# Causal masks of a forgetting attention on TensorE: mask rows loaded as weights, 64 streamed columns per mask matmul instead of 128

## The reference

```python
q = x @ Wq; k = short_conv(x @ Wk, kconv_w); v = short_conv(x @ Wv, vconv_w)   # 4 taps, then silu
q = group_rmsnorm(q, qnw, H); k = group_rmsnorm(k, knw, H)
cum = jnp.cumsum(jax.nn.log_sigmoid(x @ Wf + bf), axis=1)                      # per head
scores = jnp.einsum('bhtd,bhsd->bhts', qh, kh) * scale
scores = scores + (cum[:, :, :, None] - cum[:, :, None, :])
scores = jnp.where(causal, scores, -jnp.inf)
attn = jax.nn.softmax(scores, axis=-1)
out = jnp.einsum('bhts,bhsd->bhtd', attn, vh)
g = (x @ Wg).reshape(Bx, Tx, H, Dh)
out = out / rms(out) * onw * (g * jax.nn.sigmoid(g))
out = out.reshape(Bx, Tx, H * Dh) @ Wo
```

## Time and profile before

| | us |
|---|---|
| median of 3 runs | 2274.46 |
| lowest and highest | 2272.99, 2277.69 |
| span of the profiled execution, first to last instruction | 2273.2 |
| PE busy | 1915.3 (84 %) |
| DVE busy | 1508.8 (66 %) |
| ACT busy | 1375.1 (60 %) |
| POOL busy | 1002.6 (44 %) |

### The profile page before, as it was taken

One profiled execution on the slowest core, in us unless ns is written; L12 is line 12 of the kernel. 1 busy time (PEld: TensorE's weight loads), 2 busy tenths in 40 slices (PEclk: granted clock), 3 DMA queues, 4 the chain that ended last, 5 costly groups with the idle time before them and its releaser, 6 DMA issues. The chain is left out here.

```text
span 2273.2 us, 36182 instructions
## 1 busy us (share of the span) xinstructions
PE 1915.3 (84%) x11875; PEld 883.8 (39%) x11875; DVE 1508.8 (66%) x2281; ACT 1375.1 (60%) x2285; POOL 1002.6 (44%) x1110
## 2 busy tenths in 40 slices
PE   5468886686968758999999999999999857799996
PEld 2123333443654323444444444444444413222222
DVE  5979995794349677777778777787776536512122
ACT  3557773343344435766767767766765424699995
POOL 0167771561035314665665656656566631500001
PEclk9779997798979868999999999999999988899999
DMA  3000000000000011111121111111111100421210
GB/s 92 0 14 0 0 0 0 1 1 1 0 0 1 1 55 41 54 51 57 59 56 57 54 54 59 59 54 50 59 59 59 43 19 23 116 57 43 54 45 38
DMA packets 71430, 84.46 MB, mean 37 GB/s; under 512 B 20544, under 2 KB 44032, under 8 KB 71168
## 3 DMA queue, kind: packets, MB, share of 16 engines
q1 hardware_dynamic: 69536, 81.69, 12.3%
q10 hardware_dynamic: 1728, 0.67, 0.1%
HBM read 71.95 MB, written 9.57 MB: 36 GB/s over the span
## 5 line engine op out<-in xcount | busy, mean ns | idle before, releaser
L1690 DVE SCALAR_TENSOR_TENSOR fu_kv<-fu_ps_kv,fa_vec,fu_kv 128x511 f32<-128x511 f32 x366 | 252.8, 739 | 7.3 <-ACT fu_kv L1628 6.3
L2108 ACT ACTIVATE rt_p<-rt_ps_s 128x1024 f32<-128x1024 f32 x256 | 240.3, 1042 | 23.1 <-PE rt_ps_o L2053 17.8
L1769 POOL TENSOR_TENSOR fu_p<-fu_p 128x768 f32<-128x768 f32 x64 | 117.0, 1828 | 290.6 <-PE fu_ps_n L1475 285.4
L1445 PE MATMUL fu_ps_s<-fu_qn,fu_kn 64*128 64x512 f32 (+3 forms) x1024 | 190.9, 470 | 12.7 <-DVE fu_sg L1736 6.9
L1670 DVE TENSOR_REDUCE fu_nm<-fu_ps_m 128x2 f32<-128x1024 f32 x64 | 78.4, 1224 | 167.1 <-PE fu_ps_m L1468 167.1
L624 POOL TENSOR_TENSOR scan_hC<-scan_h,scan_c 128x1024 f32<-128x1024 f32 x64 | 150.9, 2358 | 71.7 <-DVE scan_h L600 71.7
L1475 PE MATMUL fu_ps_n<-fu_p,fu_vt 128*64 128x512 f32 (+3 forms) x1024 | 166.1, 445 | 0.0
L600 DVE TENSOR_TENSOR_SCAN scan_h<-scan_dA,scan_ps_b 128x1024 f32<-128x1024 f32 x64 | 146.4, 2287 | 2.2
L523 PE MATMUL scan_ps_y<-scan_hC,w_ident 128*128 128x512 f32 x256 | 125.5, 613 | 26.5 <-POOL scan_hC L624 14.9
L2053 PE MATMUL rt_ps_o<-rt_p,rt_va 128*32 128x512 f32 x1024 | 137.9, 610 | 10.5 <-ACT rt_p L2108 8.1
L1445 PEld LDWEIGHTS fu_ps_s<-fu_qn,fu_kn 64*128 64x128 f32 x1024 | 83.6, 186 | 133.0 <-issue 54.1
(11 more groups left out here) (368 smaller groups left out, 5037.2 us busy)
## 6 DMA issues: line engine op xcount, KB each, us to landing
fu_rb<-rms_rows SPq DMA_DIRECT2D x256, 128.0 KB, 3.0
fu_ro<-rms_rows SPq DMA_DIRECT2D x128, 128.0 KB, 2.9
ra_stackq<-rope_parts SPq DMA_DIRECT2D x168, 32.0 KB
ra_stackk<-rope_parts SPq DMA_DIRECT2D x168, 32.0 KB
w_X<-in_xT SPq DMA_DIRECT2D x4, 512.0 KB, 7.7
fa_wp<-in_wp SPq DMA_DIRECT2D x8, 256.0 KB
fa_cr<-ncum_rows SPq DMA_DIRECT2D x128, 3.0 KB
rope_parts<-ra_hi SPq DMA_DIRECT2D x16, 128.0 KB, 2.5
```

Source lines behind the costliest of these rows:

```text
L1445: pe.matmul(sps[:, h, at:at + T - t * P], k[head(h), t * P:(t + 1) * P], q[head(h), t * P:T], start=(at == 0), stop=False)
L1690: dve.scalar_tensor_tensor(acc, projected(a, k)[:, 0:T - j], vec[:, a % GA, at:at + 1], acc, ALU.mult, ALU.add).then_inc(done, 1)
L1769: pool.tensor_tensor(tail, tail, P13[:, :, 0:3 * P], ALU.add).then_inc(s.d1, 1)
L2108: act.activation(pr[k % 2][i][:, :, :], sps[(U * n + u) % RING][:, :, :], ACT.Exp, scale=DH_B ** -0.5).then_inc(s.exp, 1)
```

## The change

Before, a mask matmul loaded half an identity (64 rows, 128 columns) as weights and streamed 128 columns of mask rows. The result was a mask contribution of 128 rows and 128 columns, and the two halves j were added on the same 128 columns. Now it loads 64 mask rows (128 columns) as weights and streams an identity of 64 columns. The product is the transpose of those mask rows: 128 rows and 64 columns, so j = 0 fills the left half of the diagonal square and j = 1 the right one. As the product is transposed, `mask2` and `past2` change places.

```diff
@@ -1450,7 +1450,7 @@
                     for t, at in blocks:
                         for j in range(2):
                             for h in range(2):
-                                m = pe.matmul(sps[:, h, at:at + P], w.eye2[head(h), j, :], w.past2[head(h), j, :], start=False, stop=(j == 1 and t == blocks[-1][0]))
+                                m = pe.matmul(sps[:, h, at + 64 * j:at + 64 * j + 64], w.mask2[head(h), j, :], w.eye2[head(h), 0, 0:64], start=False, stop=(j == 1 and t == blocks[-1][0]))
                     m.then_inc(s.sc, 1)
@@ -1465,7 +1465,7 @@
                     for t, at in blocks:
                         for j in range(2):
                             for h in range(2):
-                                m = pe.matmul(mps[:, h, at + t * P:at + (t + 1) * P], w.eye2[head(h), j, :], w.mask2[head(h), j, :], start=False, stop=(j == 1 and t == blocks[-1][0]))
+                                m = pe.matmul(mps[:, h, at + t * P + 64 * j:at + t * P + 64 * j + 64], w.past2[head(h), j, :], w.eye2[head(h), 0, 0:64], start=False, stop=(j == 1 and t == blocks[-1][0]))
                     m.then_inc(s.mx, 1)
```

## The result

| us | before | changed |
|---|---|---|
| median (lowest to highest) of 4 runs each | 2275.14 (2272.99 to 2277.69) | 2261.82 (2257.86 to 2263.63) |
| span of the profiled execution | 2273.2 | 2261.1 |
| PE busy | 1915.3 | 1889.5 |
| A, median of 25 (iterations 6 to 54) | 15.628 | 15.306 |
| B, median of 26 | 14.3285 | 14.328 |

The ratio is 0.9942, with a 95% interval of 0.9924 to 0.9959: the changed kernel is faster, by 0.6 %. The two spans differ by 12.1: the stage began 2.7 later, took 12.4 less, and what lies behind it took 2.4 less. The forecast was 2262.2.

The account below looks back on a forecast made before the run. The prediction took A as bound by PE, then POOL and DVE, and B by ACT and DVE. Savings of 9.4 (A), 1.7 (first iterations) and 1.2 (last B) made 12.3 us, giving 2262.2, stated range 2254 to 2273.

Parts of the forecast that it names:

- A: Forgetting-attention iteration with output projection L1557, 15.62 us: bound by PE up to values product L1475, then by POOL and DVE.
- B: Forgetting-attention iteration between two A, without output projection, 14.33 us: bound by an ACT, then DVE chain ending at L1736.
- The price of a pair: Two mask matmuls, one per head, side by side: step time goes by streamed columns, so halving them saves 0.027 us.
- The floor: Mask steps: matmul starts at least about 25 ns apart; over both heads, 5 ns saved a pair, some 2.3 us altogether.
- A saves 12 pairs: In A, only the 12 pairs ahead of values product L1475 count: 0.32 us each, 9.4 over 29 iterations.
- B saves nothing: In B, PE arrives up to 0.43 us earlier at its end and waits for the same L1736: no saving.
- The sum: Whole attention stage: 9.4, 1.7 and 1.2 us add to 12.3 saved, taking the median to 2262.2.
- The first five iterations: Stage start: iterations 0, 1, 2 and 4 keep all 16 pairs, 4 x 0.43 = 1.7 us; 3 is like B.
- Iterations 56 to 62: Stage end: A saves 0.32 us each; B there follows POOL's chain and saves 0.3 each.
- An unchanged step: First rival, mask steps: a load or floor takes over, nothing saved, 2274.5 us; chance 0.15, a small saving included.
- a bound of PE alone: Second rival, whole stage: PE bounds everything, 64 x 0.43 = 27.6 us saved, 2246.9; chance 0.11.
- a load that waits for the drain: Third rival, mask steps: loads wait for their array half to drain, slower, about 2278 to 2361 us; chance 0.06.

Follow-up runs that it names:

- e3: Changed kernel with mask rows still as weights but the identity streaming 128 columns again: 2269.06 us, ratio 0.9993 to the kernel before.
- e4: Changed kernel with each mask matmul streaming 32 columns instead of 64, half of each diagonal square left unmasked: 2260.74 us, ratio 0.9943 to the kernel before.
- e1: Kernel before with only the score masks (L1453) narrowed to 64 columns: 2270.51 us, ratio 0.9984.
- e2: Kernel before with only the masks of the maxima (L1468) narrowed to 64 columns: 2264.53 us, ratio 0.9959.
- e12: Kernel before, old 128-column masks, with the same three moves as e11: 2298.26 us, ratio 1.0111.
- e11: Changed kernel with the moves of e8 and e9, and in B one tap behind two DVE reductions: 2280.16 us, ratio 1.0032 to the kernel before.
- e7: Changed kernel with ACT's mean squares behind its key and value copies and DVE's L1683 behind two taps: 2283.98 us, ratio 1.0051 to the kernel before.
- e5: Kernel before, old masks, with DVE's output scaling (L1719) moved right behind the queries' operation (L1677): 2265.89 us, ratio 0.9964.
- e6: Changed kernel with DVE's output scaling (L1719) moved right behind the queries' operation (L1677): 2260.55 us, ratio 0.9937 to the kernel before.
- e9: Changed kernel in which POOL, in A, waits for DVE's output scaling (L1719) before its last add (L1776): 2257.76 us, ratio 0.9935 to the kernel before.
- e8: Changed kernel with the output scaling moved behind the queries' operation in B only: 2263.3 us, ratio 0.9947 to the kernel before.

## Why the prediction was right, step by step

**The price of a pair: right.** Forecast 27 ns less; measured 27 from the records, and 0.427 of 16 pairs in each of iterations 1, 2 and 4. e3 shows that it is the columns. The floor that the third paragraph of the price took from a page of the Trainium skill ("TensorE: Matmul & The Clock Gate", "Wait — 56ns, not 53.3ns?") is near the 26 ns step of e4. Whether it or the load of 128 columns sets that step no run shows. It can't count over both heads, since both share one step of 29 ns, and so it left 27 of 27 ns here.

**A saves 12 pairs: right.** 0.322 measured, 0.32 forecast, by the chain given: POOL's wait fell by 0.32, L1719 ended 0.56 behind POOL, L1557 0.14 behind that. e1 and e2 split it into 6 and 6 pairs, and e12 against e11 shows the missing 4 come back when POOL's hold is gone. One detail was wrong: L1719 should have shrunk to 1.0, since DVE was to reach it at the old time. It kept 1.21, because L1712 ahead of it is held by POOL's L1773 in the same way (0.38, ending right behind it) and moved with POOL. In 2 of the 25 A the hold falls on the neighbour instead. One of them, DVE then PE:

```profile
1124.29 0.77 DVE L1714 TENSOR_TENSOR fa_mhl<-fu_nm,fa_mhl 128x8 bf16<-128x8 f32 x1
1124.96 0.85 DVE L1719 SCALAR_TENSOR_TENSOR fu_og<-fu_num,fu_ow,fu_ro 128x512 f32<-128x512 f32 x1
```

```profile
1125.95 1.10 PE L1557 MATMUL fu_ps_m<-fu_og,fa_wo 128*128 128x512 f32 x2 [0.37 <-DVE fu_og L1719]
```

L1776 started at 1124.28, 0.01 before L1714, which takes 0.20 elsewhere. L1719 starts 0.57 later than in the other A and ends 0.2 later, and that A takes 15.51.

**B saves nothing: right in size, wrong on where it would show.** 14.3285 and 14.328. The idle time put down to L1736 was to rise to 0.7; it stayed at 0.26, and the step from L1568 on at 0.66. PE gave its gain back earlier in B: the scores of block 2 wait for the exponential L1632, 6.86 into B where PE was ready at 6.70, and the maxima behind them wait for a reduction of DVE. Before and after:

```profile
1319.05 0.28 PE L1453 MATMUL fu_ps_s<-w_past,w_eye 64*128 64x128 bf16 x4
1319.40 0.28 PE L1461 MATMUL fu_ps_m<-fu_km,fu_qm 64*128 64x256 bf16 x2
```

```profile
1314.88 0.23 PE L1453 MATMUL fu_ps_s<-w_eye,w_mask 64*128 64x64 bf16 x4
1315.39 0.28 PE L1461 MATMUL fu_ps_m<-fu_km,fu_qm 64*128 64x256 bf16 x2 [0.29 <-DVE fu_nm L1700]
```

The maxima start 8.01 into B in all of these B of both kernels, so in the kernel before PE waited there already: from 1319.05 on are 0.35, where two mask steps take 0.11. I had looked only for the wait that ends B; there are three, and PE met the last two of them before the change and meets all three now. e7 makes the first of them bind the whole B, e5 and e6 free the chain behind it.

**The sum: 12.3 forecast, 12.4 in the stage, by other terms.** The 25 A gave 7.65, for which 25 x 0.32 says 8.0; the two of 15.51 make the difference. The first five iterations gave 3.05 instead of 1.7: 1, 2 and 4 their 0.43, 3 nothing, but iteration 0 gave 1.77. PE's first product there, before and then after:

```profile
885.27 2.08 PE L1445 MATMUL fu_ps_s<-fu_qn,fu_kn 64*128 64x512 f32 x4
```

```profile
888.01 1.13 PE L1445 MATMUL fu_ps_s<-fu_qn,fu_kn 64*128 64x512 f32 x4
```

In the kernel before, the granted clock was 0.50 (1.2 GHz) until 888.3, inside iteration 0; in the changed one it had risen at 886.3, ahead of that iteration. Old masks with the clock up take 12.46 there (e3, e12), the changed kernel 12.14, so 1.46 of the 1.77 is the clock and 0.32 the masks. This is no gain of the change: the low clock reached into iteration 0 in e5 with the old masks (13.92) and in e9 with the new (13.63) too, and both kernels have the same instructions ahead of the stage, which starts between 878 and 890 among all the kernels. Iterations 56 to 62 gave 1.72 where the forecast has 4 x 0.32 + 3 x 0.3 = 2.2 for them: 0.37, then 0.18 to 0.27 each. I had given them A's and POOL's full share without following one through. Without the clock the change is worth 12.42 - 1.46 = 10.96 in the stage, where the forecast has 12.0 for iterations 0 to 62. So the mechanism was right and the sum a little large, and a clock that rose at a lucky moment made it up. That 2262.2 and the measured 2261.82 are so close is luck as well, as the four runs of the changed kernel lie up to 5.8 apart.

**The rivals.** An unchanged step is refuted by the records, a bound of PE alone by B, a load that waits for the drain by e3 and by the 29 ns step.

## What to carry to other kernels

A matmul that adds a mask cost its streamed columns here and not its weights: put the wide matrix in the weights and the narrow identity in the stream, down to about 64 columns. Price such a saving per iteration by the wait that ends last, and count only what stands ahead of the product that this chain waits for. An operation of DVE beside an add of POOL is worth ordering by a wait: POOL's add behind it put POOL's roots off by 0.9, for which nothing waited in e9, and PE got 0.40 back per A. But ask what hangs on the add's end before a second move is built on the first.

## What the hardware showed that I had not expected

- Two mask matmuls on the two halves of the array's rows, each with a new load of 64 rows and 128 columns, take one step of 29 ns at 64 streamed columns and of 26 at 32 (e4). The load, 94 ns by its own record, never showed in a step.
- POOL's hold on DVE takes in tiny operations too: a copy of 8 columns (L1712) waits out an add of 512 columns and takes 0.38, where it takes 0.19 in B. Which of two operations that start within 0.01 gets its turn moves the chain by 0.2.
- Transfers of one form differ in how long they take to land: in e8 the write of the roots 1.3 to 3.7, with a median of 1.4, and the broadcast behind it 2.7 to 4.6, with a median of 3.0. DVE stood some 0.2 behind the usual landing, and five late ones of 26 took back what 20 had gained.
